# Causal masks of the first score pass added by TensorE in all four query chunks, none by VectorE

## The reference

```
xn  = layernorm(x)
q   = rope(xn @ wq)  16 heads of 16;   k = rope(xn @ wk), v = xn @ wv   4 key-value heads of 16
s   = q . k / sqrt(16), -inf where key position > query position      (each k, v serves 4 query heads)
att = softmax(s) @ v @ wo
ffn = real(ifft(fft(xn) @ (w_real + i w_imag))) + bias
out = x + att + ffn
```

## Time and profile before

| | us |
|---|---|
| median of 3 runs | 1133.24 |
| lowest and highest run | 1128.68, 1138.03 |
| profiled execution, span of core 0 | 1130.0 |
| TensorE busy | 1002.3 |
| VectorE busy | 866.3 |
| ScalarE busy | 692.1 |
| GpSimd busy | 184.0 |

### The profile page before, as it was taken

How to read it: one execution, slowest core, us unless ns; L and a number is a source line. 1 busy time by engine, 2 the same in 40 slices (tenths; PEclk the granted TensorE clock), 3 DMA queues, 4 the chain that set the end, 5 groups by cost and what they waited for, 6 DMA issues and landing times. The chain is left out here.

```text
span 1130.0 us, 22198 instructions
## 1 busy us (share of the span) xinstructions
PE 1002.3 (89%) x6352; PEld 410.2 (36%) x6352; DVE 866.3 (77%) x1503; ACT 692.1 (61%) x1375; POOL 184.0 (16%) x241
## 2 busy tenths in 40 slices
PE   4975499999999999999888737999999999999998
PEld 3652233333333333322556423333333333333227
DVE  6796388889898888882449836888988988888706
ACT  1451256667677777779525413666767777777882
POOL 4680021010000000000028501211100000000000
PEclk9995699999999999999989758999999999999999
DMA  7099900000000000000014994000000000000002
GB/s 218 19 148 141 124 3 1 2 1 2 1 2 1 1 2 1 2 1 2 31 48 71 144 162 54 2 2 1 1 1 2 1 1 2 1 1 2 1 1 75
DMA packets 44527, 36.01 MB, mean 32 GB/s; under 512 B 11024, under 2 KB 44432, under 8 KB 44432
## 3 DMA queue, kind: packets, MB, share of 16 engines
q1 hardware_dynamic: 44432, 34.74, 17.8%
HBM read 21.89 MB, written 12.58 MB: 31 GB/s over the span
## 5 line engine op out<-in xcount | busy, mean ns | idle before, releaser
L456 ACT ACTIVATE share<-psS 128x512 f32<-128x512 f32 (+2 forms) x1104 | 568.5, 578 | 245.5 <-PE psS L858 240.2
L637 DVE TENSOR_REDUCE pmax<-psA 128x2 f32<-128x1024 f32 x384 | 456.4, 1220 | 54.2 <-PE psA L794 52.4
L794 PE MATMUL psA<-k_st,q_st 96*128 96x512 bf16 (+3 forms) x1280 | 354.5, 360 | 35.5 <-DVE pmax L625 14.7
L858 PE MATMUL psS<-q_st,k_st 98*128 98x512 bf16 (+3 forms) x1232 | 349.8, 350 | 35.3 <-DMA q_st<-spartT 34.0
L831 PE MATMUL psO<-share,v_sb 128*32 128x512 f32 (+3 forms) x2560 | 300.0, 541 | 6.3 <-ACT share L456 3.8
L371 POOL TENSOR_SCALAR_AFFINE_SELECT share<-share 128x512 f32<-128x512 f32 x128 | 81.2, 634 | 828.2 <-ACT share L456 828.2
L858 PEld LDWEIGHTS psS<-q_st,k_st 98*128 98x128 bf16 x1232 | 113.8, 97 | 265.7 <-ACT share L456 142.0
L794 PEld LDWEIGHTS psA<-k_st,q_st 96*128 96x128 bf16 x1280 | 110.3, 100 | 239.5 <-DVE pmax L637 77.4
L633 DVE CUSTOM_DVE_ANT_0 psA<-psA,mask 128x128 f32<-128x128 f32 (+3 forms) x256 | 119.0, 516 | 20.9 <-PE psA L794 20.9
L625 DVE TENSOR_REDUCE pmax<-psA 128x4 f32<-128x512 f32 (+2 forms) x96 | 98.9, 1042 | 22.8 <-PE psA L797 22.5
L831 PEld LDWEIGHTS psO<-share,v_sb 128*32 128x32 f32 x2560 | 50.4, 108 | 108.2 <-ACT share L456 55.3
(11 more groups left out here) (84 smaller groups left out, 631.4 us busy)
## 6 DMA issues: line engine op xcount, KB each, us to landing
q_st<-parts_scratch SPq DMA_DIRECT2D x48, 256.0 KB, 8.8
parts_scratch<-share SPq DMA_DIRECT2D x8, 1024.0 KB, 11.8
x_sb<-in_L_attn_x SPq DMA_DIRECT2D x8, 512.0 KB, 8.2
out<-x_sb SPq DMA_DIRECT2D x8, 512.0 KB, 3.0
k_st<-parts_scratch SPq DMA_DIRECT2D x48, 64.0 KB, 12.4
q_st<-spartT SPq DMA_DIRECT2D x128, 2.0 KB
share<-dft_tables SPq DMA_DIRECT2D x1, 512.0 KB, 4.1
share<-in_L_ffn_w_freq_real SPq DMA_DIRECT2D x1, 256.0 KB, 4.4
```

What stands on the lines that cost most here:

```text
L456: nc.scalar.activation(prob[:, u % 2, k * hp:(k + 1) * hp, s0:CH], score_bank(tail, bank)[:, 0:hp * w].rearrange("p (h s) -> p h s", h=hp) ...
L637: nc.vector.reduce_max(pmax[:, heads[0]:heads[0] + 2, i, q], psA[:, two:two + 2, :], AX.X).then_inc(S["a_reduced"], 1)
L794: last = mm(psA[:, 2 * (v % 2) + k // per, (k % per) * w:(k % per + 1) * w], q_st[0:ROWS, n, r, i * P:(i + 1) * P], k_st[0:ROWS, g, q * CH ...
L858: last = mm(score_bank(tail, bank)[:, h * w:(h + 1) * w], k_st[0:ROWS + SHIFT, g, tile * P:(tile + 1) * P], q_st[0:ROWS + SHIFT, nl, k * h ...
```

## The change

`PE_MASKS` goes from 8 to 16, so that TensorE adds the mask in all steps. VectorE's add-and-maximum branch, the fp32 mask, the two GpSimd instructions that write it, and a semaphore that only this branch counted up are removed; the numbers of `const_ready` are adapted.

```
-        mask = sb("mask", [P, CH], fp32)
...
-        PE_MASKS = 2 * KV
+        PE_MASKS = STEPS
...
-            nc.gpsimd.memset(mask[:, :], 0.0).then_inc(S["const_ready"], 1)
...
-            pool.wait_ge(S["const_ready"], 7)
+            pool.wait_ge(S["const_ready"], 6)
...
-            nc.gpsimd.affine_select(out=mask[:, :], in_=mask[:, :], compare_op=ALU.is_ge, fill=NEG, base=CH - P,
-                                    pattern=[[-1, CH]], channel_multiplier=1).then_inc(S["const_ready"], 1)
...
-            pool.wait_ge(S["const_ready"], 12)
+            pool.wait_ge(S["const_ready"], 10)
...
-                    elif q == n // KV:
-
-                        dve.sem_inc(S["scores_seen"], 1)
-                        for k, r in enumerate(heads):
-                            scores = psA[:, two + k // per, (k % per) * w:(k % per + 1) * w]
-                            last = nc.vector.tensor_tensor_reduce(scores, scores, mask[:, CH - w:CH], 1.0, NEG,
-                                                                  ALU.add, ALU.max, pmax[:, r, i, q:q + 1])
-                        last.then_inc(S["a_reduced"], 1)
...
-            pe.wait_ge(S["const_ready"], 12)
+            pe.wait_ge(S["const_ready"], 10)
```

More of the change, by code:

```diff
@@ L128, in attention_fourier_block @@
             "o_transposed", "rl_ready", "o_normed", "on_transposed", "onT_ready", "wo_done", "out_ready", "out_stored",
-            "unit_seen", "stats_seen", "scores_seen")}
+            "unit_seen", "stats_seen")}
         x_in = [sem(f"x_in{c}") for c in range(NJ)]
```

## The result

| | before | after |
|---|---|---|
| median of 12 runs, us | 1134.57 | 1139.88 |
| lowest to highest | 1128.68 to 1138.03 | 1136.60 to 1145.58 |
| profiled span | 1130.0 | 1137.0 |

The ratio is 1.0051, 95% interval 1.0034 to 1.0068: about 6 us slower, which is real, and within the 1% that the prediction took for no change. The forecast was 1139.2 us and +0.5%.

What follows compares the result with a forecast made beforehand. TensorE was taken to bound the two attention stretches. 15.4 - 8.4 - 1.0 = +6.0 us, added to the median 1133.24, gave 1139.2 us (+0.5%); own range 1133 to 1146, with rivals 1130 to 1149.

Steps and rivals of the forecast that it cites:

- What bounds: In the two stretches where masks move, TensorE sets the pace (277.06 of 283 us busy); VectorE has some 12% to spare.
- Added on TensorE, +15.4: Chunks 2 and 3: 256 more mask matmuls at 0.06 us from start to start, +15.4 us, half in each batch.
- Removed from VectorE, 24.6 us real time: Diagonal groups of chunks 2 and 3: 24.6 us less by start distances, 56 at most by records; worth nothing by itself.
- Holes, -8.4: TensorE's waits ahead of first-pass scores, 17.4 us in all: 8.4 us regained, ends 0 and -17.4.
- The worked hole: TensorE's wait before the score matmul at 232.00 us, predicted to shrink from 0.96 to 0.55 us.
- 0.2 us a hole: Gain assumed for each of 21 holes in each of two batches, giving -8.4 us.
- its first rival: The rival "Nothing is regained": under 4 us of the holes close, +14.4 us, 1147.7 us; chance 0.20.
- The start, -1.0: Kernel start: without GpSimd's fp32 mask memset and select, VectorE's chain and TensorE begin 1.0 us sooner; ends 0 and -1.0.
- Nothing is regained: Chunks 2 and 3: later diagonal reductions replace the removed VectorE wait; +14.4 us, 1147.7 us; chance 0.20.
- Weight loads: Identity loads on TensorE cannot hide, 0.098 us per mask, 25.1 us; sum +15.7, 1148.9 us; chance 0.04.
- VectorE was the hidden pace: With 25 us less work VectorE is never late and all holes close: -3.0 us, 1130.2 us; chance 0.12.
- What would show it: Signs: stretches 3 to 4 us longer, TensorE idle 2 or 3 us, 192 reductions, first normalisation 1 us earlier.

Runs made afterwards that it cites:

- the doubled masks: The changed kernel with each mask matmul of chunks 2 and 3 issued twice; ratio 1.0174 to the kernel before, 1.0122 over the changed kernel.
- the groups of four alone: The kernel before with masks of chunks 2 and 3 on TensorE only where four heads share a use; ratio 1.0034 to the kernel before.
- the kernel with the cost and no relief: The kernel before with TensorE masking every diagonal tile while VectorE keeps its add-and-maximum in chunks 2 and 3; ratio 1.0110 to the kernel before.
- relief alone: The kernel before with no first-pass mask in chunks 2 and 3, VectorE taking the plain maximum; ratio 0.9948 to the kernel before.

## Why the prediction was right, step by step

- **What bounds.** Right for the stretches. Adding masks makes the time longer, doubling them again, and taking work from VectorE alone gives back 2.3 us a batch of the 8.5 in the holes. The order of TensorE's other matmuls is the same in both traces, as said. (The description of the planner ahead of the prediction has one thing wrong: 1.0 is `a_weight` of a full use; a diagonal one has 0.7 to 1.2 by its width. It does not ask who masks either way.)
- **Added on TensorE, +15.4.** The start distance of 0.06 us is there in the new places, and the doubled masks confirm it. The 81 ns of the Trainium skill (TensorE: Matmul & The Clock Gate, Back-to-back issue gap) do not fit: of the 512 masks after the change 430 have 0.058 to 0.060 us to the next start, and 63 have 0.106 or 0.107, in chunks 0 and 1, where the granted clock is at its lower level.
- **Removed from VectorE, 24.6 us real time.** Its busy time fell by 20.6 us, near the estimate from start distances and far from the 56 of the summed records, which count overlapping operations twice.
- **Holes, -8.4.** 15.4 - 2 x 3.51 = 8.4 us were regained, in both ways that the prediction named: about 3.7 by masks inside waits (2 x 1.84) and 4.5 by relief (2 x 2.26). The worked hole went to 0.40 us, not 0.55: the old group started 0.19 us after the scores' record and the new one 0.04 after the masks', and that latency had been overlooked. With the semaphore instruction put back it is 0.51 us. The count "0.2 us a hole" was a choice between 0 and all; that it came out to the tenth is luck. The balance of one group, by which the prediction argued against its first rival, does not tell how much is given back: with the groups of four alone, half of the masks kept half of the cost.
- **The start, -1.0.** Right on the average of ten traces (0.97), but only 0.3 in the profiled pair, because of where TensorE's clock rose. The sum of the two, 7.0 - 1.0 = 6.0, lies by the ratio's 5.8 us; the medians are 5.3 apart. In the profiled pair the start gives 0.3 us and the stages between take 0.3 more, so that 7.0 us are left between the spans.
- **The rivals.** *Nothing is regained* (1147.7) would have needed the kernel with the cost and no relief, and even that one gets nearly 4 us back. *Weight loads* and *VectorE was the hidden pace* are excluded by the doubled masks and by relief alone, which leaves 6.2 us of holes: ahead of 9 of its 15 VectorE had itself waited for TensorE before its last reduction, and the others follow the small operations that end a step.
- **What would show it.** Idle down to 2 or 3 us (3.0), stretches 3 to 4 us longer (3.5), 192 reductions: met. The first normalisation 1 us earlier was not met in this pair.

## What to carry to other kernels

Price a small matmul by the distance from its start to the next, not by its record, and ask of every stretch separately who is late: moving the 128 masks of a batch to TensorE cost 3.5 us in chunks 2 and 3, where TensorE was the bound, and the 64 of chunk 1, where VectorE would have been late, saved 2.6, of which 1.7 through TensorE's clock. Read the clock column before a difference is put down to waits: in the two runs that took masks off chunk 1 the granted clock was at its lower level for longer. When work moves from an engine with slack to the one that bounds, count the bound engine's holes and expect about their share that lies behind the moved work, no more. Before one pair of traces is believed on a term of a microsecond, look at a few executions: where the clock rises can hide it.

## What was not expected of the hardware

A memset over two partitions (6.92 us for 2 x 8192 bf16 elements) held an fp32 operation of VectorE for 6.1 us longer than its own 0.43 us, and moving it by one wait was worth nearly as much as the mask's place (4.3 us less, against 5.3 more for the change). Operations on layer-norm statistics beside the same memset were not slowed (5.33 us for 16, and 5.32 without it). An instruction that only takes a wait and counts up a semaphore delays the work behind it by 0.11 us.
